# Turning the row of maxima two heads later in the four-step units, and loading and summing w2 and w3 at other places, in a one-core transformer layer

## The reference

```python
x = x + attention(layernorm(x))      # 16 heads of 16 features, causal, with ALiBi bias
x = x + ffn(layernorm(x))
scores = q @ k.T / sqrt(16) + slope[h] * distance[key]; masked where key > query
attn = softmax(scores); ctx = attn @ v; return ctx @ Wo + bo
# ffn: sigmoid(h @ t(w1).T) * (h @ t(w2).T), and its product with t(w3).T
# t(w) = clip(round(w / (mean(|w|) + 1e-8)), -1, 1)
```

## Time and profile before

| what | value |
|---|---|
| time, median of 3 runs | 640.15 us (639.23 to 640.62) |
| profiled execution, device time | 635.68 us |
| its span | 634.0 us |
| PE busy | 592.9 us, 94% |
| DVE busy | 462.2 us, 73% |
| ACT busy | 362.2 us, 57% |
| POOL busy | 187.6 us, 30% |
| mean granted clock of PE | 0.994 |

### The profile page before, as it was taken

One profiled execution on the slowest core, in us unless ns is written; L12 is line 12 of the kernel. 1 busy time (PEld: TensorE's weight loads), 2 busy tenths in 40 slices (PEclk: granted clock), 3 DMA queues, 4 the chain that ended last, 5 costly groups with the idle time before them and its releaser, 6 DMA issues.

```text
span 634.0 us, 10885 instructions
## 1 busy us (share of the span) xinstructions
PE 592.9 (94%) x3488; PEld 369.9 (58%) x3488; DVE 462.2 (73%) x1198; ACT 362.2 (57%) x774; POOL 187.6 (30%) x396
## 2 busy tenths in 40 slices
PE   7877788999999999999999999999999999999887
PEld 5554445565667574655656666556555566565487
DVE  5976988577878885677887887888888888311176
ACT  3446447655654456666465464577666674766521
POOL 7636522261341242340212321221200300423300
PEclk9999999999999999999999999999999999999989
DMA  6886743742313126331141130362312110001001
GB/s 193 261 250 169 204 122 86 202 149 72 88 35 102 36 66 202 125 98 38 37 119 34 41 97 2 93 182 77 96 51 69 55 35 1 19 29 43 0 18 34
DMA packets 27453, 57.52 MB, mean 91 GB/s; under 512 B 5316, under 2 KB 14916, under 8 KB 23940
## 3 DMA queue, kind: packets, MB, share of 16 engines
q1 hardware_dynamic: 27396, 56.82, 32.0%
HBM read 40.69 MB, written 14.80 MB: 88 GB/s over the span
## 4 chain that ended last, share of the span: by engine, by line
PE 74%; DVE 16%; issue 5%; ACT 4%; DMA 1%; POOL 0%; ACTq 0%; POOLq 0%
PE pO L1091 20%; PE pS L1078 19%; PE pM L1057 16%; PE pM L1032 5%; DVE pm L1258 5%; DVE pM L1261 3%; PE pM L969 3%; PE pM L1040 2%; ACT probs L895 2%; PE pM L1018 2%; PE pM L977 2%; PE pS L1032 1%; PE pS L969 1%; PE pS L1040 1%; DMA qst<-mT 1%
## 5 line engine op out<-in xcount | busy, mean ns | idle before, releaser
L895 ACT ACTIVATE probs<-pS 128x512 f32<-128x512 f32 (+3 forms) x640 | 300.1, 545 | 171.7 <-PE pS L1078 169.8
L1258 DVE TENSOR_REDUCE pm<-pM 128x1 f32<-128x512 f32 x384 | 239.1, 680 | 46.0 <-PE pM L1057 45.6
L1078 PE MATMUL pS<-qst,kst 128*128 128x512 f32 (+3 forms) x640 | 245.2, 403 | 6.4 <-ACT probs L895 3.8
L1057 PE MATMUL pM<-kst,qst 126*128 126x512 f32 (+3 forms) x640 | 227.0, 384 | 9.3 <-DVE pm L1261 4.2
L1078 PEld LDWEIGHTS pS<-qst,kst 128*128 128x128 f32 x640 | 118.5, 189 | 95.7 <-issue 48.5
L1261 DVE CUSTOM_DVE_ANT_0 pM<-pM,mask 128x128 f32<-128x128 f32 (+3 forms) x256 | 119.7, 522 | 39.7 <-PE pM L1057 39.3
L1057 PEld LDWEIGHTS pM<-kst,qst 126*128 126x128 f32 x640 | 119.6, 190 | 48.6 <-DVE pm L1258 12.7
L775 POOL TENSOR_SCALAR_AFFINE_SELECT probs<-probs 128x128 f32<-128x128 f32 x256 | 77.9, 317 | 218.7 <-ACT probs L895 211.1
L1091 PE MATMUL pO<-probs,vals 128*17 128x512 f32 (+3 forms) x1280 | 133.3, 531 | 0.0
L1091 PEld LDWEIGHTS pO<-probs,vals 128*17 128x17 f32 x1280 | 29.9, 96 | 64.7 <-issue 40.3
L764 POOL CAST hT<-work 128x256 fp32r<-128x256 f32 (+1 forms) x34 | 13.5, 397 | 90.6 <-DVE work L1224 71.3
(11 more groups left out here) (158 smaller groups left out, 424.8 us busy)
## 6 DMA issues: line engine op xcount, KB each, us to landing
kst<-parts SPq DMA_DIRECT2D x78, 256.0 KB
qst<-parts SPq DMA_DIRECT2D x30, 256.0 KB, 4.0
parts<-qk_hl SPq DMA_DIRECT2D x28, 256.0 KB, 4.6
ctx_dram<-ctx_raw SPq DMA_DIRECT2D x15, 256.0 KB, 3.7
xin<-in_L_attn_x SPq DMA_DIRECT2D x5, 512.0 KB, 5.1
out<-work SPq DMA_DIRECT2D x8, 256.0 KB, 4.2
work<-ctx_dram SPq DMA_DIRECT2D x7, 256.0 KB
work<-rden_dram SPq DMA_DIRECT2D x7, 256.0 KB
```

The source lines that it names most:

```text
L895: nc.scalar.activation(probs[:, n % PSLOTS, q0:CH], pS[:, n % SBANKS, q0:CH], ACT.Exp)\
L1057: pe.matmul(max_bank(x)[:, 0:N], qst[0:R_MAX, u % QSLOTS, h, t * P:(t + 1) * P], kst[0:R_MAX, n % KSLOTS, h, 0:N], start=True, stop=True). ...
L1078: pe.matmul(pS[:, n % SBANKS, q0:CH], kst[0:R_END, sl, h, b:b + P], qst[0:R_END, u % QSLOTS, h, q0:CH], start=True, stop=True).then_inc(sc ...
L1258: nc.vector.tensor_reduce(dst, bank, AX.X, ALU.max).then_inc(max_free, 1)
```

## The change

Three things are moved, and nothing is computed otherwise. In units of four steps the swap stands after head 2 instead of head 0 of the last but one step; that is behind `weighted` for two steps, which also stands after head 2. On SP, the two DMAs of w2 stand ahead of the first `load_m`. On ACT, the sum of w2 stands after step 0 instead of step 1, and that of w3 inside step 2, after head 1 and its side group, instead of at the end of step 2. In the head, the second piece of the projection Q10 stands before the first swap.

```diff
-    swap_in = {first_step[u] - 2: u for u in range(1, NU)}
+    swap_in = {(first_step[u] - 2, 0 if n_steps[u - 1] > TPC else 2): u for u in range(1, NU)}
 
     def swap_after(s, h):
-        return swap_in.get(s) if h == 0 else None
+        return swap_in.get((s, h))
@@ sync
             store_parts(("q", 0, 1))
+            load_raw(1, w2)
             load_m(0)
             load_k(2)
             load_q(2)
             store_parts(K10)
             store_parts(Q10)
-            load_raw(1, w2)
@@ scalar
                     if h == SIDE_AFTER and side[s]:
                         side_op(side[s])
+                    if (s, h) == (2, SIDE_AFTER):
+                        size_of_weights(2)
                 if j == 0 and u >= 1:
                     save_ctx(u - 1)
-                if s in (1, 2):
-                    size_of_weights(s)
+                if s == 0:
+                    size_of_weights(1)
@@ tensor
+            side_group(Q10, 1)
             swap_max(0)
-            side_group(Q10, 1)
```

## The result

The changed kernel takes 635.34 us (median of 4 runs, 634.74 to 635.62) against 640.38 (639.23 to 641.42) for the kernel before, run beside it: the ratio is 0.992, with an interval of 0.9902 to 0.9939. That is 5.0 us less; 3.9 were forecast (636.2). The lines of the changed kernel bear numbers two higher (scores L1080, turns L1059, swap L1067).

The account below looks back on a forecast made before the run. PE, busy 94%, was taken as the bound, early gains limited by DVE's idle time. 0 + 0.3 + 1.35 + 1.3 + 1.0 = 3.95, 3.9 off the 640.15 median: 636.2 us; likeliest case 634.7 to 637.8, 8 in 10 633.8 to 640.2.

Parts of the forecast that it names:

- The head: Before unit 0: Q10's piece, at most 0.6 us, fits PE's 1.70 us wait; w2's load delays nothing; cost 0.
- The rule of ring order: Head: descriptors go in ring order, so mT's packets can't pass w2's; price nothing or little, +2.5 us if wholly colliding.
- Unit 1: Swap in step 2: first scores at 51.6 instead of 51.93 us, net gain 0.3 us.
- gamma's 1.22 us are won and lost again to mT's DMA: Unit 1: PE's wait for w3's sum goes, but a new 1.3 us wait for mT comes before the first scores.
- Unit 2: Step 6: DVE's waits of 0.87 and 0.89 us for late turns go, 0.4 kept back; gain 1.35 us.
- Unit 3: Step 10: DVE's waits of 0.70 and 1.19 us shrink to about 0.6 together; gain 1.3 us.
- DVE sets the time there, and I count nothing for it: Unit 3: the low clock, 0.93, in that window may go too, but was given 0 gain.
- its waits only move: Rival, units 2 to 4: DVE's waits shift to where the ring of four is full, a quarter remains, 0.9 us; chance 0.22.
- Unit 4: Step 14: PE's 1.66 us wait goes, scores at 102.6 instead of 103.75 us; gain taken as 1.0.
- The rival of the late row: Units 1, 2 and 4: the row of maxima lands 2 us later, 5 us lost against 3.9 gained, 641.2; chance 0.15.
- DVE is the bound anyway: Rival, units 1 to 4: DVE's little idle time limits the gain to 1.2 us, 638.9 us; chance 0.22.

Follow-up runs that it names:

- 4: Kernel before with only the second piece of Q10 moved ahead of the first swap: 642.04 us, ratio 1.0017.
- 7: Changed kernel with the second piece of Q10 put back behind the first swap: 632.41 us, ratio 0.9891.
- 8: Changed kernel with unit 1's swap back after head 0 of step 2: 634.97 us, ratio 0.9917.
- 10: Changed kernel with PE's waits filled by unread transposes and unit 1's swap back early: 631.2 us, ratio 0.9848.
- 3: Kernel before with only w2's load and the sums of w2 and w3 moved: 637.68 us, ratio 0.9947.
- 6: Changed kernel with unread transposes of the identity in PE's waits and at unit 2's swap: 630.44 us, ratio 0.9859.
- 5: Kernel before, in its order, with unread transposes before the five swaps and unit 0's first scores: 635.11 us, ratio 0.9924.
- 11: Changed kernel with waits filled, unit 3's swap back early and 16 transposes before it instead of 15 in step 10: 631.39 us, ratio 0.9861.
- 2: Kernel before with only the swaps of units 1 to 4 moved two heads later: 634.76 us, ratio 0.9905.
- 9: Changed kernel with 15 unread transposes in step 10's wait alone, ahead of the side group: 630.62 us, ratio 0.9846.

## Why the prediction was right, and where it was not

In short: the swaps of units 2 and 4 brought what was told, and a little more; unit 3's brought almost nothing; unit 1's gain came from the sums. That the total was near is in part luck, as the sum below shows.

**The head: the time held, the piece was mis-sized.** First scores of unit 0 at 35.84 both times. The rule of ring order that stood against w2's place had almost nothing to bite on: w2's share was 0.73 until 34 and 0.16 for half a microsecond more, mT's DMA was issued to the queue until 34.05, and it landed 2.55 us behind the start of its issue, as before. 0 was taken, of bounds 0 to +2.5. Q10's piece took 0.85 us and not at most 0.6. At equal clock that costs nothing (-0.2 us off the line), but PE then stands 0.65 us longer for mT, and what followed for the clock (4 and 7) the prediction left out.

**Unit 1: a gain of 0.3 forecast, 0.3 in the profile and 0.4 where neither side has a low stretch in the unit (16.09 to 15.69), by another way than was told.** `gamma`'s wait went and the path of mT was sized right, 3.11 us for 3.17. What failed is the step "gamma's 1.22 us are won and lost again to mT's DMA". The first scores are not what unit 1's length hangs on. Experiments 8 and 10 moved them 0.5 and 0.4 us forward from the negation and gained 0.1 and 0.0. The gain comes from the loads and sums alone: with the swap still early, in 3, the unit takes 15.68 us. The 0.8 that 6 less 5 gives has w2's later landing in 5 in it.

**Unit 2: 1.35 forecast, 1.7 measured.** The mechanism is as told: the waits of 0.87 and 0.89 us in the earlier trace rows are gone, 0.20 and 0.17 remain, and the row of maxima was not late. 16.15 to 14.41 us between the two profiles, neither of them low in this unit; 6 less 5 gives only 0.8, because 0.9 us of 6 are its own filling. Against the usual execution of before it is 3.2 us (17.64 to 14.41), since the wait of 3 us in which the clock fell goes too.

**Unit 3: 1.3 forecast, 0.1 to 0.2 measured, the step that failed.** It said "DVE sets the time there, and I count nothing for it". With the swap early and the wait before it filled, so that PE comes out of it at the full clock (5 and 11), the wait of 0.70 us in the earlier trace rows is not there at all: it came from turns made at the low clock behind 77, and before with its waits filled needs 21.06 us for the unit where 21.98 were read. The other, 1.19, is 1.06 there, and the late swap exchanges it for 0.64 at the copy. So 0.4 us was to be won, not 1.3, and 0.1 to 0.2 came. And the wait of PE did not go, it moved: from the swap (2.19) to the transposes of step 10 (2.16), where it brought the low clock of 75 to 82. In after the profile shows 23.09 us, 1.1 *longer* than the good execution of before. Filling that wait gave 2.2 us back. The rival "its waits only move" had this unit right, with PE where it had named DVE.

**Unit 4: 1.0 forecast, 1.3 measured where neither side is low.** First scores at 103.42 (about 100 forecast) with a wait of 0.23 for mT (0.3 forecast). Against 103.75 in the earlier trace rows they come only 0.3 us sooner, since unit 3 gave nothing and the low stretches at 75 and 95.5 took their part. With step 10 filled they come at 99.93. The unit's own length is the cleaner measure. Before took 28.56 us with no low stretch in the unit, and five kernels with the late swap took 27.20 to 27.28 without one (2, 6, 7, 8 and 9); 10, whose low stretch ends 0.6 us ahead of the unit, took 27.62. The 28.25 of after has the stretch at 95.5 to 98.9 partly in it, and the 29.06 of 5 the filling that held back its swap.

**The sum.** 3.9 us was forecast, and 5.0 came (before and after as they run), 4.2 (at one clock) and 4.7 (with the waits filled). Added up by units, each taken where the low clock is in neither side (in unit 3, 5 less 6, with the low stretch at the end of 5's unit), the order gave 0.4 + 1.7 + 0.1 + 1.3 = 3.5 us. The size is near, but the terms were not these: 1.2 us too much in unit 3 and 0.3 to 0.4 too little in each of units 2 and 4, and these errors all but cancel, which is luck. The forecast also left out the clock. The other 1.5 of the 5.0 us go with low stretches, of which the usual execution of before has more (mean clock 0.985 for 0.987); how they share out was not measured. That the shift would be subtracted from the median and not from 635.68 was right for a reason that the prediction did not give: the profiled execution stood at a clock of 0.994, the usual one at 0.985. Subtracting from the execution would have given 631.8, which after reached in none of its four runs. The rival of the late row fell in all of units 0 to 4 (waits for mT of at most 0.73 us besides unit 0's), and with it "DVE is the bound anyway" as a sum, though not in unit 3.

**Open.** The filled kernels' medians lie 4.7 us apart, their profiled executions 3.6, of which 3.4 are there by the negation for unit 5. The profiled execution of 5 is the fastest of its six, so the last 1 us lies in executions of 5 of which no trace was kept. Why the stretches at 95.5 and 218 come and go. And what Q10's piece costs through the clock: a kernel with step 10 filled and the piece left behind the swap was not run, nor one with 6's filling less the products at the swap for unit 2.

## What to carry to other kernels

Before you subtract from a profile, see how its mean granted clock stands to that of the other runs: here one profiled execution was 4.7 us better than the usual one. A wait in a ring of buffers does not vanish by moving one user of the ring; look for the next instruction that needs a place, and for what its wait does to the engine's clock. Here a few idle products that nobody reads, put into the waits, gave the kernel before 5.0 us, as much as the reordering did, and the changed kernel 4.7 us more; put where there was no wait, they cost 0.9 us.

## What the runs showed of the hardware

- In or behind waits of PE the granted clock fell to about 0.5, for 3 to 7 us: in one of 2.16 us in step 10 of after, in one of 2.94 us before the swap for unit 2 in one execution of before, and not in one of 3.04 us at the same place in another. It also fell where no wait of over 0.7 us stood near (95.5 and 218 in after, 94.1 in 5), so the length of the last wait does not foretell it here. The Trainium skill ("TensorE: Matmul & The Clock Gate", section "HAM oscillation — how this bites in real kernels") tells of a kernel whose clock swings because PE waits for data between bursts, and advises an order of loops that keeps PE busy. The traces agree in kind for the longer waits: where they were filled, the mean clock went to 0.996 and more.
- The same program takes 642 us at a mean clock of 0.980 and 636 at 0.995. By the line that is 3.3 us for 0.01 of clock. Over 634 us, 0.01 of clock is 6.3 us of PE's work at full speed; half of it shows in the time. Where the other half goes was not looked at.
- With a single wait of 2.2 us filled by 15 transposes of 1.80 us together, the kernel took 4.7 us of 635 less, more than the stall itself; 2.2 us of it are in the unit of that wait.
- The DMA of the row of maxima, 16 KB, landed 2.55 us after its issue began, with 0.7 MB issued 4.5 us ahead of it on the same queue or with none.
